# Experts of a transformer layer on one core: gathered rows turned by DMA into a ring of four, gathers eight ahead

## The reference, cut to what matters

```python
x = x + _L0_xattn_ref(_layernorm(x), ctx_1024, ...)   # 2048 rows of 256: causal attention, cross attention, FFN
x = x + _L0_ffn_ref(_layernorm(x), wg, w1, w3, w2)    # 8 experts, the best two for each row

def _L0_ffn_ref(hidden_states, wg, w1, w3, w2):
    x = hidden_states.reshape(-1, H)
    probs = jax.nn.softmax(x @ wg.T, axis=-1)
    topk_w, topk_idx = jax.lax.top_k(probs, 2)
    topk_w = topk_w / jnp.sum(topk_w, axis=-1, keepdims=True)
    expert_w = jnp.sum(jax.nn.one_hot(topk_idx, E) * topk_w[..., None], axis=1)
    h1 = jnp.einsum('th,eih->tei', x, w1)
    h3 = jnp.einsum('th,eih->tei', x, w3)
    y = jnp.einsum('tei,ehi->teh', jax.nn.silu(h1) * h3, w2)
    return jnp.einsum('te,teh->th', expert_w, y).reshape(hidden_states.shape)
```

## Time and profile before

| | us |
|---|---|
| three runs | 534.71, 536.51, 536.86 |
| their median | 536.51 |
| the profiled execution | 538.54 |
| its span | 536.7 |
| PE busy in the span | 500.5 (93%) |
| POOL busy in the span | 288.0 (54%) |

### The profile page before, as it was taken

How to read it: one execution, slowest core, us unless ns; L and a number is a source line. 1 busy time by engine, 2 the same in 40 slices (tenths; PEclk the granted TensorE clock), 3 DMA queues, 4 the chain that set the end, 5 groups by cost and what they waited for, 6 DMA issues and landing times.

```text
span 536.7 us, 10988 instructions
## 1 busy us (share of the span) xinstructions
PE 500.5 (93%) x3686; PEld 326.6 (61%) x3686; DVE 378.5 (71%) x968; ACT 286.5 (53%) x574; POOL 288.0 (54%) x324
## 2 busy tenths in 40 slices
PE   7999999999899999898999988899998999999990
PEld 3676766666667666566666764556655656666660
DVE  6899887588877678858977989788857544444440
ACT  4556867655648637654647557455544334433430
POOL 4464112004724519936696875343566665766663
PEclk9899999999999999999999999899999999999996
DMA  8002534246887357763697770226885677878973
GB/s 278 7 31 70 171 94 120 84 107 118 145 173 143 109 110 132 160 165 109 106 213 158 145 259 11 69 65 124 142 155 100 116 120 136 126 126 123 139 91 40
DMA packets 135314, 65.61 MB, mean 122 GB/s; under 512 B 109757, under 2 KB 126590, under 8 KB 135262
## 3 DMA queue, kind: packets, MB, share of 16 engines
q1 hardware_dynamic: 127774, 54.69, 45.9%
q0 software_dynamic: 7488, 10.23, 12.8%
HBM read 28.19 MB, written 10.35 MB: 72 GB/s over the span
## 4 chain that ended last, share of the span: by engine, by line
PE 51%; DVE 16%; DMA 11%; issue 8%; ACT 6%; POOL 4%; POOLq 2%; SPq 1%; DVEq 0%; ACTq 0%
PE ps L1197 41%; DMA out<-y,qst 6%; DMA probT<-prob 3%; PE ps L1292 3%; PE ps L1294 3%; PE ps L1293 3%; DVE cmax L1735 2%; ACT ps L1008 1%; POOL y L935 1%; DVE tT L1944 1%; POOLq L955 1%; DVE prob L1876 1%; DVE arena L394 1%; POOL out L961 1%; DVE arena L468 1%
## 5 line engine op out<-in xcount | busy, mean ns | idle before, releaser
L1197 PE MATMUL ps<-arena,probT 128*128 128x256 f16 (+2 forms) x1092 | 179.6, 318 | 3.5 <-DMA probT<-prob 2.2
L1197 PEld LDWEIGHTS ps<-arena,probT 128*128 128x128 f16 (+1 forms) x1092 | 104.8, 97 | 60.7 <-issue 7.0
L961 POOL DMA_INDIRECT out<-y,qst x39 | 62.7, 1608 | 23.6 <-DMA out<-y,qst 12.9
L1197 PE MATMUL ps<-arena,qT 128*128 128x512 f16 (+1 forms) x384 | 68.9, 332 | 1.6 <-DVE prob L1876 1.2
L1007 ACT ACTIVATE prob<-ps,nbias 128x512 f16<-128x512 f32 x64 | 39.0, 609 | 53.3 <-DVE nbias L1741 53.3
L2296 DVE SCALAR_TENSOR_TENSOR ps<-ps,w1m 128x512 f32<-128x512 f32 x39 | 27.4, 703 | 53.5 <-ACT w1m L1138 51.0
L1138 ACT ACTIVATE w1m<-ps 128x512 f32<-128x512 f32 x39 | 23.3, 597 | 76.9 <-PE ps L1197 63.8
L1197 PE MATMUL ps<-arena,tT 128*128 x468 | 57.3, 273 | 0.6 <-DVE tT L2395 0.6
L776 POOL TENSOR_TENSOR rstd<-veps,expo 128x1 f32<-128x1 f32 x16 | 9.2, 573 | 88.0 <-DVE veps L1770 88.0
L1197 PEld LDWEIGHTS ps<-arena,qT 128*128 128x128 f16 x384 | 32.4, 97 | 37.1 <-issue 3.2
L1197 PE MATMUL ps<-w2s,tT 128*128 128x256 f16 x384 | 47.6, 274 | 3.4 <-DVE tT L1944 3.0
(11 more groups left out here) (232 smaller groups left out, 920.4 us busy)
## 6 DMA issues: line engine op xcount, KB each, us to landing
stage<-we_in SPq DMA_DIRECT2D x33, 256.0 KB, 3.1
prob<-we_in SPq DMA_DIRECT2D x15, 256.0 KB, 3.7
xin<-x_in SPq DMA_DIRECT2D x16, 128.0 KB, 2.8
out<-y SPq DMA_DIRECT2D x16, 128.0 KB
hrow<-tT SPq DMA_DIRECT2D x4, 512.0 KB, 3.3
y<-x_in SPq DMA_DIRECT2D x3, 512.0 KB, 7.2
stage<-z_in SPq DMA_DIRECT2D x4, 256.0 KB, 5.5
prob<-w_in SPq DMA_DIRECT2D x4, 256.0 KB, 2.8
```

Source lines behind the costliest of these rows:

```text
L961: g.indirect_dma_start(out[:rows_of(p), :], bass.IndirectOffsetOnAxis(ridx[:, n:n + 1], 0), ys[:, n % RING, :], None, compute_op=ALU.add). ...
L1197: r = t.matmul(o, lhs(a), rhs(b), start=first and n == 0, stop=last and n == 2)
```

## The change

x_trans, x_copy and their semaphores (e_xtr, e_xcp) are gone. In their place SP issues one DMA with transpose per tile, `x_turn`, of 128 x 512 float16, from `xg` into `xT`, which now has four places and lies where the FFN's first weights were (`w1m`); it therefore waits until the FFN's last up-product (f_up) has been made. x_turn(n) for n from 4 on waits for e_ups of tile n - 4, whose place it takes, and for its gather. e_ups(n) waits for the landing of x_turn(n) (e_t0 to e_t3), and a gather for that of the tile four before.

On SP, x_turn(0) to x_turn(3) stand behind store_h(2), and then x_turn(n + 4) stands ahead of act_turn(n). On POOL the gathers are issued up to tile n + 7 in turn n of the loop, at most two in a turn, those of the second phase from turn 3 on and those of the third from turn 11 on.

```diff
-RING, AHEAD, BEHIND = 4, 6, 3
-LEAD = 2
+RING, AHEAD, BEHIND = 4, 8, 3
+GATHERS_FROM = {1: 3, 2: 11}
+MOST = 2
...
-        xT = ph[:, 4096:5120].rearrange("p (q b c) -> p q b c", q=2, b=2 * KD)
+        xT = w1m[:, 2 * NI:].bitcast(F16).rearrange("p (s b c) -> p s b c", s=RING, b=2 * KD)
...
+            def x_turn(n):
+
+                s = n % RING
+                if n < RING:
+                    wait(sp, "f_up", KF * NB)
+                else:
+                    wait(sp, "e_up", n - RING + 1)
+                wait(sp, f"e_x{s}", 16 * (n // RING + 1))
+                sp.dma_start_transpose(xT[:, s], xg[:, s, :]).then_inc(sm[f"e_t{s}"], 16)
+
...
             store_h(sp, 2)
+            for n in range(RING):
+                x_turn(n)
             for n in range(NJ):
+                if n + RING < NJ:
+                    x_turn(n + RING)
                 if n < NJ - 1:
                     act_turn(n)
...
             def gather(n):
                 if n >= RING:
-                    wait(pool, "e_xtr", n - RING + 1)
+                    wait(pool, f"e_t{n % RING}", 16 * (n // RING))
...
-            issued = AHEAD - 1
+            issued = 5
             for n in range(NJ):
-                while issued < min(NJ, n + AHEAD + (LEAD if n > PHASES[2][1] - AHEAD + 1 else 0)):
-                    gather(issued)
-                    issued += 1
+                for _ in range(MOST):
+                    if issued < min(NJ, n + AHEAD) and n >= GATHERS_FROM.get(phase_of(issued), 0):
+                        gather(issued)
+                        issued += 1
...
-            def x_copy(n, q):
-                act_.wait_ge(sm["e_xtr"], n + 1)
-                copy(xT[:, q, :, :].rearrange("p b c -> p (b c)"), x_bank(n)).then_inc(sm["e_xcp"], 1)
...
-            def x_trans(n, s):
-                pe.wait_ge(sm[f"e_x{s}"], 4 * (n - s) + 16)
-                for b in range(2 * KD):
-                    r = t.transpose(x_bank(n)[:, b * P:(b + 1) * P], xg[:, s, b * P:(b + 1) * P],
-                                    ident16[:])
-                r.then_inc(sm["e_xtr"], 1)
...
             def e_ups(n, q):
                 at = expert[n]
-                pe.wait_ge(sm["e_xcp"], n + 1)
+                s = n % RING
+                pe.wait_ge(sm[f"e_t{s}"], 4 * (n - s) + 16)
...
-                if nxt:
-                    x_trans(n + 1, (s + 1) % RING)
                 if n == BEHIND + 1:
                     routing_read(2)
```

More of the change, by code:

```diff
@@ L322, in xattn_ffn_moe @@
             h_out x1_out fill_out r_count r_tab r_next r_made r_listed r_list chain links_p
-            e_x0 e_x1 e_x2 e_x3 e_a0 e_a1 e_a2 e_a3 e_xtr e_xcp e_up e_sil e_act e_ahi e_alo e_down e_y
+            e_x0 e_x1 e_x2 e_x3 e_a0 e_a1 e_a2 e_a3 e_t0 e_t1 e_t2 e_t3 e_up e_sil e_act e_ahi e_alo e_down e_y
             e_add0 e_add1 e_add2 e_add3 e_ltr e_lcp""".split()
@@ L572, in last_bank @@
             return ps[2 - 2 * ((NJ - 1) % 2) + a][:].bitcast(F16)[:, :CH]
[L574 to L578, removed]
         block = ctx.enter_context(nc.Block())
@@ L1144, in act_hi, with e_step @@
                 copy(arow[:, s, 0, :], ps[2 * (s % 2) + 1][:]).then_inc(sm["e_ahi"], 1)
-            def e_step(n, s, nxt=True):
+            def e_step(n, s):
                 silu(n, s % 2)
-                if nxt:
-                    x_copy(n + 1, 1 - s % 2)
                 act_hi(n, s)
@@ L1161, in weighted @@
                 a.activation(ys[:, s, :], psO[s % 2][:, :D], ACT.Copy, scale=rgate[:, n:n + 1]).then_inc(sm["e_y"], 1)
-            x_copy(0, 0)
             h_copy(2, 0)
-            x_copy(1, 1)
             h_copy(2, 1)
             silu(0, 0)
-            x_copy(2, 0)
             act_hi(0, 0)
@@ L1171, in _ @@
                 silu(n, n % 2)
[L1172 to L1175, removed]
                 if n == H_AT:
@@ L1183, in _ @@
             for n in range(E_LOOP, NJ):
-                e_step(n, n % RING, n + 1 < NJ)
+                e_step(n, n % RING)
             wait(act_, "e_ltr", 1)
@@ L1544, in e_ups @@
                     for k in range(KD):
-                        r = mm3(ps[2 * q + h][:], lambda a: xT[:, q, a * KD + k, :],
+                        r = mm3(ps[2 * q + h][:], lambda a: xT[:, s, a * KD + k, :],
                                 lambda b: ew[:, at + (k * 2 + h), b, :], k == 0, k == KD - 1)
@@ L1573, in _ @@
             down(3, 5)
-            wait(pe, "f_lo", KF * NB - 2)
-            x_trans(0, 0)
             wait(pe, "r_list", 1)
@@ L1578, in _ @@
             down(3, 6)
-            wait(pe, "f_lo", KF * NB - 1)
-            x_trans(1, 1)
             h_trans(2, 1)
@@ L1587, in _ @@
             wait(pe, "st_lo", G_FF + len(rest))
-            wait(pe, "e_xcp", 2)
             e_ups(0, 0)
             wait(pe, "n_u", NT)
-            x_trans(2, 2)
             wait(pe, "r_lg", NB - 1)
             e_ups(1, 1)
-            x_trans(3, 3)
             ranks(2)
@@ L1604, in routing_read, with e_step @@
                 wait(pe, "r_used", j - (NB - 3) + 1)
-            def e_step(n, s, nxt=True, between=None, banks=None):
+            def e_step(n, s, between=None, banks=None):
                 q = s % 2
@@ L1637, in _ @@
             for n in range(2, E_LOOP):
-                e_step(n, n % RING, n > 2, work.get(n), read.get(n - 1))
+                e_step(n, n % RING, work.get(n), read.get(n - 1))
             for n in range(E_LOOP, NJ - 1):
```

## The result

| us | before | after |
|---|---|---|
| median of four runs | 536.68 | 545.83 |
| lowest and highest | 534.71, 538.89 | 542.70, 547.53 |
| profiled execution, its span | 538.54, 536.7 | 542.70, 541.0 |

The changed kernel is slower: ratio 1.0141, 95% interval 1.0092 to 1.0191, some 7.6 us on 536.5. The two medians of the table lie further apart, 9.15 us (1.0170), so the size is known to some 2 us only. The profiled execution of after is the fastest of its four and that of before is 2 us above its median, so the two traces differ by 4.3 us of span only.

A forecast was written before the change was run, and what follows sets the result against it. The end was taken to hang on POOL's chain of adds, not PE. The terms 0 + 0.35 - 1.4 + 5.0 + 0 gave +3.95 us, 540.5 us against a median of 536.51; range for 8 in 10, 530 to 550.5 us.

The forecast's parts named there:

- What bounds the kernel: Expert part: POOL's chain of adds sets the end, 159.2 us; POOL lags behind PE's results, 4.2 us at the end.
- Part 1: PE and ACT: 39 x_trans of 0.22 us and 39 copies go; PE's 8.6 us shorten nothing, 0.
- Part 2: Prelude up to the first add: act_turn(0) comes late behind x_turn(4), +0.35 us, between -0.7 and +2.
- Part 3: POOL's gathers: the interval with three gathers between adds 11 and 12 goes, -1.4 us, 0 to -2.5.
- Part 4: DMA engines: 39 more transfers lengthen 20 awaited landings of adds by 0.25 us each, +5.0 us, 0 to +14.6.
- first rival: Not slower: no landing of an add gets longer, 535.5 us, band 533.5 to 538; chance 0.2.
- Part 5: SP: x_turn's gather wait holds up act_turn, a loop of 9.7 to some 13 us that the chain covers, 0.
- third rival: Much slower: the DMA engines or the loop through SP set the pace, about 550 us, band 544.5 to 556; chance 0.18.
- forecast case: Awaited landings of adds get longer by 0.13 to 0.45 us, 538 to 544.5 us; chance 0.45.
- The second: Rival: faster, because PE sets the end after all, at most 8.6 us, 527.9 us, band 525 to 533.5; chance 0.17.
- What would show it: Signs in the profile after: 20 or more landing waits, over 39.5 us together, and PE idle some 8 us.
- Wrong altogether: Sign against the forecast: adds wait for DVE's weighted, the lag gone; the end then hangs on PE or SP's loop.

The follow-up runs named there:

- idle transposes: The kernel before with added transposes that nobody reads, without x_turn's gather wait: 1.0133 ahead of act_turn, 1.0194 behind it, 1.0082 behind it with the new gather order.
- the run behind act_turn: The kernel before with added transposes of x_turn's size that nobody reads, each behind its act_turn, old gather order: 1.0194.
- the one wait: The kernel before with unread transposes at x_turn's place, 1.0133; the same with x_turn's wait for its gather added, 1.0271.
- the one order: The changed kernel with act_turn(n) ahead of x_turn(n + 4) on SP, 1.0037; the changed kernel measured again as it is, 1.0183.
- the second measurement: The changed kernel measured once more, unaltered, against the kernel before: 1.0183.
- act_turn first: The changed kernel with act_turn(n) ahead of x_turn(n + 4) on SP: 1.0037.
- act_turn first and a quarter: The changed kernel with act_turn(n) ahead of x_turn(n + 4) and x_turn moving one block of 128 columns of four: 0.9958.

## Why the prediction was right in sign and short in size

**What bounds the kernel** was right as far as it says that PE doesn't: with the transposes taken out and nothing put in their place, the time is the same, so PE's 20.00 of 20 us was no bound. That the chain of adds on POOL set the end of the kernel before is what remains, and no run shortened that chain by itself.

**Part 1, PE's 8.6 us at 0**: right, 0.9987 without them. The step became 3.90 us, as worked out.

**Part 2, the prelude**: forecast +0.35 us, first add near 369.6. It was at 368.48, -0.8 us; act_turn(0) did hold up PE, 1.87 us at 365.61. Its lower bound was -0.7, and one execution doesn't tell the two apart.

**Part 3, the gathers**: -1.4 us. Alone -0.8 us, with an interval of -2.8 to +1.2. What the term left out is that with traffic on the engines the order is worth 0.9 to 1.1%, some 5 us: the step took the gathers for a length on POOL and not for what PE and SP need in time (how that comes to lengthen the chain is open).

**Part 4, the traffic**: +5.0 us of chain. The idle transposes gave +5.8 and +8.3 us with the old gathers, and +3.5 us in all with the new ones (162.8 - 159.2), where the sum had 5.0 - 1.4 = 3.6. The size was near, but not by the way it was reached. The term was to be a longer wait at each of 20 landings. The waits for landings, 39.5 us before, are 41.5, 44.3 and 39.2 us in these three runs, 40.2 and 34.8 in the two traces of the changed kernel, so only the run behind act_turn has the 5 us there. The rest of what the traffic costs lies elsewhere in the loop, and the fit of the size is in part luck. The first rival's time has fallen (1.0133 and 1.0194 with nothing but the transposes, 1.0082 with the new gathers).

The rule in the Trainium skill, "Advanced Engine Details and Errata", section "X-Bar Transpose (TRN2)", that transposing DMAs are as fast as regular ones, would have made this term smaller by 2.3 us. The chain grew by more than either figure, 5.8 us, with 39 idle transposes of 128 KB in the kernel before (7 us of its time); no run moved the same bytes by plain DMAs, so these runs don't test the rule by themselves. The trace's comparison in the prediction is rougher than it looks, too: in the window of 386 to 387 an add and a gather of POOL were under way beside the plain stores.

**Part 5, the loop through SP at 0: this step failed.** It went from 1.0133 to 1.0271 for the one wait, and from 1.0037 to 1.0183 for the one order, 7 to 8 us each (5.6 us by the first measurement of the changed kernel, 1.0141). Without it the changed kernel is 2 us slower than before (0.4 to 3.7), where the sum had +3.95; so the excess over the forecast is this step. The part named the mechanism and the instructions, and then said that the chain covers it and that PE has 8.6 us to give. Two figures in it did not hold.

The loop was put at 9.7 to some 13 us. For tile 21 in after it can be read off whole: gather(25), x_turn(25), act_turn(21), e_downs(21) and weighted(21):

```profile
452.26 1.00 POOL L944 DMA_INDIRECT y<-hrow,qst  x1 [0.31 <-issue]
...
457.16 1.21 SPq L689 DMA_TRANSPOSE w1m<-y  x1
458.46 1.81 SPq L697 DMA_TRANSPOSE tT<-prob  x1
```

```profile
464.47 2.74 PE L1194 MATMUL ps<-arena,tT 128*128 x12 [2.30 <-DMA tT<-prob]
...
467.25 0.48 DVE L2292 TENSOR_SCALAR y<-ps,qst 128x256 f32<-128x256 f32 x1 [3.71 <-PE ps L1194]
```

The gather took 4.90 us to the transpose's start (3.1 was taken, 5 named as its limit), x_turn 1.30, act_turn 5.87 us to land where 3.4 was taken, e_downs with its lowered clock 2.74 in place of 1.47: from 452.26 to 467.73, 15.5 us. The durations were those of quiet stretches, in a kernel whose engines part 4 had just filled. And gather 17, which can't go before turn 11, is issued ahead of add(10), a turn later than the loop assumed.

For tile 21 the cover held: its add still went 4.9 us after the result. What the wait cost was PE's time, and with it the lag of the tiles behind.

PE's 8.6 us were the other figure. The stops for act_turn took 12.8 us, and behind two of them the clock fell: 1.27 + 1.61 us longer at 427.98, and 1.27 + 0.45 at 464.47 (e_ups took 3.20 us in place of 2.75), 4.6 us. That is 17.4 us out of a saving of 8.6, a loss of 8.8. It agrees with the end of the trace: the last result stood at 524.28 before and stands at 532.28, 8.0 us later. The lag at the end, 4.2 us before and 0.45 now, could pay for 3.8 of these, and the last add is 4.2 us later. From tile 32 on the adds went 0.3 to 2.3 us after their results, so PE's side set the end.

**The rivals.** The result, 545.83, lies in the band of the third rival, 544.5 to 556, which was given 0.18, and not in that of the forecast case. The third named this loop (x_turn ahead of act_turn) beside full DMA engines, but its 550 us were worked out from the engines alone, and those workings have fallen: an interval of the chain is 4.32 us in after (164.3 / 38) and not 4.6, and the waits for landings did not grow by 14.6 us. That the lag paid for some 4 us of the loop fits its end in the trace, but no run took the lag away by itself, so it is argued and not shown. The second is excluded by the kernel without transposes.

**What would show it.** Landings waited for at the gap 2.0 us, 1.8 in the second measurement (forecast 1.9): right. Over 39.5 us of them together: 40.2 in one trace and 34.8 in the other, not borne out. 20 or more waits: 18, wrong, and this was the first sign. PE idle in front of e_downs, some 8 us: 12.8. DMA share over 0.9: 0.95 to 1.03. "Wrong altogether" were adds that wait for DVE's weighted, a lag gone to nothing: that came in the last tiles, and it points to the step that failed.

## What to carry to other kernels

A transfer that is put into an in-order queue ahead of one that somebody waits for passes its own wait on to it; put it behind, which cost two lines here and gave back 1.5% of 1.8%. Before calling a slack a cover, add up all that will be drawn from it, with the durations of a loaded stretch, and see whether it lasts to the end of the chain. Work taken off an engine that the end doesn't hang on gave nothing here (0.9987), while what replaced it cost time on the path. A size that comes out right is no proof of the way it was reached: look for the term's own waits in the trace.

## What was not expected of the hardware

- A stop of PE costs more than its length: behind stops of 4.79 and 2.30 us the granted clock stood at 0.52 for 6 us and at 0.50 for 3 us, and the matmuls there took up to 1.9 times as long (2.74 against 1.47 us). In the second trace of the changed kernel the same lower level followed a stop of 3.65 us (e_downs 2.74 us), and with act_turn first one of 3.11. Behind stops of 2.05 us (at 495.65) and 1.87 us (at 365.61) in after it did not fall, 1.00 in the windows behind them.
- A transpose of a quarter of the size holds SP for nearly as long: 1107 ns at the least for 128 columns (in the kernel with act_turn first and a quarter), 1189 for 512 and 1234 for 1024 in after. On SP it costs by number; on the DMA engines the quarter was the cheaper one, 1.0043 against 1.0183.
- An act_turn that lands in 3.4 us in a quiet stretch took 4.4, 5.9 and 6.1 us in the three pieces of the chain.
